# Fp8 rounding in four VectorE operations over a PSUM bank, the clip at the head loads, q/k normalisation on ScalarE, one bank for q/k turns

## The reference

```python
ln_out = ln(layernorm(x)) * ln_w + ln_b
q  = fp8_linear(ln_out, wq)    # 16 heads of 128;  k, v: 8 heads;  qx: 16 heads
kx, vx = split(ctx @ w_kv_x.T) # 8 heads each
q, qx, k, kx = each head normalised over its 128 columns, * weight + bias
core = softmax(q k' / sqrt(128)) v          # 8 groups, 2 query heads per group
xout = softmax(qx kx' / sqrt(128)) vx
catq = fp8(bf16(clip(concat(core, xout) / proj_smooth, -448, 448)))
x = x + catq @ wproj.T * scale
x = x + ffn(layernorm(x))                   # gate/up/down, hidden width 1408
```

## Time and profile before

| | before |
|---|---|
| median of 3 runs | 2063.76 us |
| profiled execution, its own time | 2065.24 us |
| its span | 2063.4 us |
| mean granted TensorE clock | 0.977 |
| PE busy | 1719.0 us (83%) |
| DVE busy | 1648.0 us (80%) |
| ACT busy | 1226.5 us (59%) |
| POOL busy | 1223.0 us (59%) |

### The profile page before, as it was taken

One profiled execution on the slowest core, in us unless ns is written; L12 is line 12 of the kernel. 1 busy time (PEld: TensorE's weight loads), 2 busy tenths in 40 slices (PEclk: granted clock), 3 DMA queues, 4 the chain that ended last, 5 costly groups with the idle time before them and its releaser, 6 DMA issues.

```text
span 2063.4 us, 48409 instructions
## 1 busy us (share of the span) xinstructions
PE 1719.0 (83%) x15776; PEld 1233.5 (60%) x15776; DVE 1648.0 (80%) x3887; ACT 1226.5 (59%) x2158; POOL 1223.0 (59%) x1045
## 2 busy tenths in 40 slices
PE   0016989998998989898889989898999776999998
PEld 0015767776776777676667767776777543444443
DVE  8996999999899989998998999899999732223132
ACT  2244767777666777776677767676788733131211
POOL 3454777777777777777676777776877611120202
PEclk9998999999999999999999999999999888999999
DMA  4100866776777677677867766876788894030200
GB/s 148 40 30 1 139 113 121 150 140 109 124 122 139 116 126 142 118 132 131 139 111 129 141 117 120 136 141 113 124 164 167 189 278 174 6 118 29 93 20 20
DMA packets 639388, 240.92 MB, mean 117 GB/s; under 512 B 612496, under 2 KB 612496, under 8 KB 638608
## 3 DMA queue, kind: packets, MB, share of 16 engines
q1 hardware_dynamic: 639120, 237.62, 57.8%
HBM read 65.57 MB, written 20.97 MB: 42 GB/s over the span
## 4 chain that ended last, share of the span: by engine, by line
DVE 35%; issue 30%; PE 21%; ACT 6%; POOL 3%; SPq 1%; DMA 1%; DVEq 1%; ACTq 0%; POOLq 0%
PE ps_pj L557 8%; DVE local L1050 4%; DVE sq_sum L1121 3%; DVE local L1059 3%; DVE local L1046 3%; DVE local L1178 3%; DVE local L1055 2%; DVE local L1198 2%; POOL local L958 2%; DVE w_raw L1008 2%; DVE local L1140 2%; PE ps_o L626 2%; PE ps_o L628 2%; PE ps_o L627 2%; DVE neg_max L1168 2%
## 5 line engine op out<-in xcount | busy, mean ns | idle before, releaser
L557 PE MATMUL ps_pj<-wide 128*128 (+2 forms) x5544 | 596.5, 256 | 102.6 <-DVE local L1140 82.9
L942 POOL TENSOR_TENSOR local<-local 128x512 bf16<-128x512 f32 x512 | 619.7, 1211 | 78.7 <-ACT local L812 78.3
L557 PEld LDWEIGHTS ps_pj<-wide 128*128 128x128 bf16 x5544 | 466.0, 99 | 250.4 <-DVE local L1140 92.4
L809 ACT ACTIVATE local<-ps_s,neg_max 128x512 f32<-128x512 f32 x512 | 355.1, 693 | 380.8 <-DVE neg_max L1168 378.6
L920 POOL TENSOR_TENSOR head_rstd<-head_var,minus_half 128x3 f32<-128x3 f32 x256 | 247.1, 965 | 339.5 <-DVE head_var L1126 336.8
L626 PE MATMUL ps_o<-v_hi,local 128*128 128x129 bf16 x2048 | 382.9, 224 | 38.4 <-DMA local<-local 25.2
L628 PE MATMUL ps_o<-v_hi,local 128*128 128x129 bf16 x2048 | 382.6, 221 | 0.0
L627 PE MATMUL ps_o<-local 128*128 128x128 bf16 x2048 | 382.2, 220 | 0.0
L1168 DVE TENSOR_REDUCE neg_max<-ps_s 128x1 f32<-128x512 f32 x512 | 344.6, 673 | 44.8 <-PE ps_s L642 42.8
L812 ACT ACTIVATE local<-ps_s,neg_max 128x512 bf16<-128x512 f32 x512 | 352.2, 688 | 15.4 <-DMA local<-local 15.3
L927 POOL TENSOR_TENSOR local<-local 128x512 bf16<-128x512 f32 x192 | 245.9, 1281 | 4.3 <-ACT local L764 4.2
(11 more groups left out here) (99 smaller groups left out, 2866.6 us busy)
## 6 DMA issues: line engine op xcount, KB each, us to landing
w_raw<-w_group SPq DMA_DIRECT2D x32, 512.0 KB, 4.2
quantised_heads<-local SPq DMA_DIRECT2D x32, 512.0 KB, 3.2
wide<-quantised_heads SPq DMA_DIRECT2D x4, 4096.0 KB, 13.8
local<-local SPq DMA_TRANSPOSE x640, 3.3
local<-x SPq DMA_DIRECT2D x4, 1024.0 KB, 5.3
local<-ctx_t SPq DMA_DIRECT2D x4, 1024.0 KB, 5.1
w_raw<-w_proj SPq DMA_DIRECT2D x8, 512.0 KB, 4.1
wide<-w_proj SPq DMA_DIRECT2D x4, 1024.0 KB, 6.2
```

The lines of the kernel that those rows point to most:

```text
L557: last = mm(dst[:, at:at + n], lhs, w_at(par, part, c, cross * 512 + at, n), start=(k == 0), stop=(k == len(terms) - 1))
L809: a(p_exp[:, u % 2], ps_s[u % 2][:], ACT.Exp, bias=neg_max[:, u % 4:u % 4 + 1])
L942: tt_(pp[:, u % PP_BUFS, 1], p_exp[:, u % 2], pp[:, u % PP_BUFS, 0], ALU.subtract)\
```

## The change

- `clip` leaves the slots. The loaded `heads_in` are clipped instead, 128x16384 bf16 in one VectorE operation per batch (`clip_heads`): for batch 0 in slot 65 of the last group, for batches 1 to 3 in the middle of the feed-forward block of the batch before. The output projection waits for `clipped` where it waited for `heads_back`.
- The other four operations: the exponent bits into `mag` (SBUF), max with 2^-6 and min with 256 into the PSUM bank `ps_y` (fp32), and two scalar_tensor_tensor operations that multiply `ps_y` by 24 or -24 and add. Three of them stand at lag 6 and the last at lag 8 (before: 8 and 10); the head's transpose and store are two slots earlier.
- `head_norm` moves from VectorE to ScalarE, as three copies of 128 columns with a per-row scale, behind the exponentials of the odd slot.
- `ps_y` takes the place of the second `ps_qt` bank. Every turn waits for the full copy of the turn before. The bf16 copy stands in the turn's own slot (`QK_LAG` 0), the full copy in the next (`FULL_LAG` 1).
- Weight sums run over six of the eight heads and scaling over seven; the weight steps are one slot later.

```diff
-        ps_qt = [psum(f"ps_qt{i}") for i in range(2)]
+        ps_qt = psum("ps_qt")
+        ps_y = psum("ps_y")
...
-        PV_LAG, Y_LAG, QUANT_LAG, QUANT_END_LAG, HEAD_LAG, STORE_LAG = 5, 6, 8, 10, 11, 13
+        PV_LAG, Y_LAG, HEAD_LAG, STORE_LAG = 5, 6, 9, 11
...
-        QK_LAG, REST_LAG = 1, 3
+        QK_LAG, FULL_LAG, REST_LAG = 0, 1, 3
+        QUANT_LAG, QUANT_END_LAG = 6, 8
...
-        SUMS_LAG, SCALE_LAG, SCALE_PIECES, W_HI_LAG, W_LO_LAG = 2, 4, 2, 8, 10
+        SUMS_LAG, SCALE_LAG, SCALE_PIECES, W_HI_LAG, W_LO_LAG = 3, 5, 2, 9, 11
...
+        CLIP_SLOT = HEADS_SLOT + 6
...
 def turn_qk(q, j, n, tiles):
-                if not isinstance(n, int) or n >= 2:
-                    pe.wait_ge(full_done, n - 1)
+                pe.wait_ge(full_done, n)
...
-                pe.wait_ge(heads_back, 16 * (b + 1))
+                pe.wait_ge(clipped, b + 1)
...
 ScalarE
+            def head_norm(i, t, turns):
+                act.wait_ge(rstd_done, t + 1)
+                if not isinstance(t, int) or t >= TILES:
+                    act.wait_ge(qt_done, turns)
+                for h in range(3):
+                    hs = slice(h * D, (h + 1) * D)
+                    last = a(qn[:, i, hs], tile_bank(i, t)[:, hs], ACT.Copy, scale=head_rstd[:, i % 2, h:h + 1])
+                last.then_inc(qn_done, 1)
...
+            def qk_high(q, j, n):
+                act.wait_ge(qt_done, n + 1)
+                b, cross = quad_place(q)
+                w, bias = qk_columns(q, j)
+                a(qk_hi[:, b, cross, HEAD_OF_TURN[j]], ps_qt[:], ACT.Identity, bias=bias, scale=w)
+
+            def qk_whole(q, j, n):
+                if not isinstance(n, int) or n >= 2:
+                    act.wait_ge(qklo_done, n - 1)
+                w, bias = qk_columns(q, j)
+                a(qk_full[:, (q + j) % 2], ps_qt[:], ACT.Identity, bias=bias, scale=w).then_inc(full_done, 1)
...
 ScalarE, group(), behind the exponentials of the slot
+                    for k in tile_at(slot, QN_LAG, first, last):
+                        head_norm(tile_place(k)[1], GROUP_TILES * g + TILES + k, GROUP_TURNS * g + 3 * (1 + k // TT))
                     for q, j in turn_at(slot, QK_LAG, first, last):
-                        qk_part(q, j, GROUP_TURNS * g + 3 * (2 + q) + j)
+                        qk_high(q, j, GROUP_TURNS * g + 3 * (2 + q) + j)
+                    for q, j in turn_at(slot, FULL_LAG, first, last):
+                        qk_whole(q, j, GROUP_TURNS * g + 3 * (2 + q) + j)
...
 VectorE
+            def clip_heads(b):
+                dve.wait_ge(heads_back, 16 * (b + 1))
+                v.tensor_scalar(heads_in.rearrange("p g h t -> p (g h t)"), heads_in.rearrange("p g h t -> p (g h t)"),
+                                FP8_MAX, -FP8_MAX, ALU.min, ALU.max).then_inc(clipped, 1)
...
                     for H in head_at(slot, QUANT_LAG, first):
-                        binade(B * CH + GROUP_HEADS * g + H, y[:, H % 2], mag)
+                        dve.wait_ge(y_done, SLOTS * g + TT * (H + 1) + UNIT_FREE)
+                        v.tensor_scalar(mag.bitcast(I16), y[:, H % 2].bitcast(I16), EXPONENT, None, ALU.bitwise_and)\
+                            .then_inc(binade_done, 1)
+                        dve.wait_ge(binade_done, GROUP_HEADS * g + H + 1)
+                        v.tensor_scalar(ps_y[:], mag, MIN_BINADE, MAX_BINADE, ALU.max, ALU.min).then_inc(mag_done, 1)
+                        dve.wait_ge(mag_done, GROUP_HEADS * g + H + 1)
+                        v.scalar_tensor_tensor(summed, ps_y[:], KEEP4, y[:, H % 2], ALU.mult, ALU.add).then_inc(total_done, 1)
                     for H in head_at(slot, QUANT_END_LAG, first):
...
+                        v.scalar_tensor_tensor(heads_n[:, H % 2], ps_y[:], -KEEP4, summed, ALU.mult, ALU.add)\
+                            .then_inc(heads_done, 1)
...
 VectorE, hidden()
+                    if m == HC // 2 and clip_next is not None:
+                        clip_heads(clip_next)
```

More of the change, by code:

```diff
@@ L48 @@
 KEEP4 = 24.0
+MAX_BINADE = 256.0
 PP_BUFS = 4
@@ L255, in block_kernel @@
         y_done = sem("y_done")
+        binade_done = sem("binade_done")
+        mag_done = sem("mag_done")
+        total_done = sem("total_done")
+        clipped = sem("clipped")
         heads_done = sem("heads_done")
@@ L750, in v_part, with qk_columns, qk_part @@
                 a(v_hi[:, b % 2, i // TT, i % TT, 0:D], tile_bank(i, t)[:, 3 * D:4 * D], ACT.Copy).then_inc(vhi_done, 1)
-            def qk_part(q, j, n):
+            def head_norm(i, t, turns):
[6 more added lines that the diff above has]
+                last.then_inc(qn_done, 1)
+            def qk_columns(q, j):
+                cross = q % 2
+                if j == 0:
+                    return (c_("kxln_w"), c_("kxln_b")) if cross else (c_("kln_w"), c_("kln_b"))
+                return qscaled[:, 2 * cross:2 * cross + 1], qscaled[:, 2 * cross + 1:2 * cross + 2]
+            def qk_high(q, j, n):
                 act.wait_ge(qt_done, n + 1)
+                b, cross = quad_place(q)
+                w, bias = qk_columns(q, j)
+                a(qk_hi[:, b, cross, HEAD_OF_TURN[j]], ps_qt[:], ACT.Identity, bias=bias, scale=w)
+            def qk_whole(q, j, n):
                 if not isinstance(n, int) or n >= 2:
                     act.wait_ge(qklo_done, n - 1)
[L757 to L764, removed]
+                w, bias = qk_columns(q, j)
+                a(qk_full[:, (q + j) % 2], ps_qt[:], ACT.Identity, bias=bias, scale=w).then_inc(full_done, 1)
+            def qk_part(q, j, n):
+                qk_high(q, j, n)
+                qk_whole(q, j, n)
             scale_chunk(B - 1, 0)
@@ L779, in _ @@
                     v_part(0, i, i)
+                    head_norm(i - 1, i - 1, 0)
                 if i == START_TURN:
@@ L782, in _ @@
                         qk_part(-2, j, j)
+            head_norm(TILES - 1, TILES - 1, 0)
             for j in range(3):
@@ L996, in weight_sums @@
                 dve.wait_ge(w_loaded, 16 * (count + FREE))
[L997 removed]
+                v.tensor_reduce(w_sum[:].rearrange("p (s k) -> p s k", s=2)[:, :, 0:3],
+                                raw(c).rearrange("p (s k d) -> p s k d", s=2, k=4)[:, :, 0:3], AX_X, ALU.add).then_inc(w_step, 1)
                 dve.wait_ge(w_step, 2 * count - 1)
@@ L1005, in weight_scale @@
                 n = 8 // SCALE_PIECES
-                for k in range(n * piece, n * (piece + 1)):
+                for k in range(n * piece, min(n * (piece + 1), 7)):
                     head = raw(c)[:, k * D:(k + 1) * D]
@@ L1133, in v_rest @@
                                 v_hi[:, b % 2, i // TT, i % TT, 0:D], ALU.subtract).then_inc(vlo_done, 1)
[L1135 to L1143, removed]
             quantise_chunk(B - 1, 0, True)
@@ L1169, in group @@
                             .then_inc(max_done, 1)
-                    for H in head_at(slot, QUANT_LAG, first):
-                        clip(B * CH + GROUP_HEADS * g + H, y[:, H % 2])
                     for u in unit_at(slot, Y_LAG, first):
@@ L1189, in group @@
                         head_variance(tile_place(k)[1], GROUP_TILES * g + TILES + k)
[L1190 to L1198, removed]
                     for piece in range(SCALE_PIECES):
@@ L1208, in group @@
                         v.reciprocal(rows, rows).then_inc(smooth_ready, 1)
+                    if last and slot == CLIP_SLOT:
+                        clip_heads(0)
             group(0, True, False)
@@ L1241, in output, with hidden @@
                     v.tensor_tensor(y_out[:, tt % 2], scaled[:, tt % 2], x1_at(b, tt), ALU.add).then_inc(out_ready, 1)
-            def hidden(b):
+            def hidden(b, clip_next):
                 for tt in range(TT):
@@ L1255, in hidden @@
                                            ALU.mult, ALU.mult).then_inc(hid_done, 1)
+                    if m == HC // 2 and clip_next is not None:
+                        clip_heads(clip_next)
             residual(0, [*EARLY_BANKS, ps_s[EARLY_TILES % 2]])
-            hidden(0)
-            with dve.Fori(1, B) as b:
+            hidden(0, 1)
+            with dve.Fori(1, B - 1) as b:
                 residual(b, ps_s * 2)
                 output(b - 1)
-                hidden(b)
+                hidden(b, b + 1)
+            residual(B - 1, ps_s * 2)
+            output(B - 2)
+            hidden(B - 1, None)
             output(B - 1)
```

16 lines of the change are left out of this document (8 added, 8 removed).

## The result

The changed kernel took 2230.83 us (median, 2227.8 to 2237.54), the kernel before 2065.02 us beside it: a ratio of 1.08, 95% interval 1.0763 to 1.0838. The direction was forecast, the size was not: 2160 us was forecast with a range to 2220, and +166 us was measured against +96.

A forecast was written before the change was run, and what follows sets the result against it. VectorE was taken to bound the kernel before, and a serial chain through ScalarE the changed one. Main stage +86, start +5, first clip +4 and other clips +1 gave +96 us, so 2160 us, range 2085 to 2220.

The forecast's parts named there:

- VectorE's relief: Main stage: moving head_norm and cheaper rounding cut VectorE's work from 176 to about 144 us per group.
- The chain: Serial waits from scores through ScalarE's exponentials and copies to scores two slots on: 189.2 us per group.
- what comes on top of the chain: Main-stage extras per group: 3.4 us on VectorE plus 4.5 us, making a group 197.1 us.
- late work on VectorE: VectorE late for a maximum: 2.4 us at the slot-31 reciprocal plus 1 us for weight pieces, per group.
- the rest: Return of the loop to its first slot and late transposes: 4.5 us per group (0 to 6).
- Weight pieces that meet a rounding add 1 us: VectorE in the main stage: weight steps meeting rounding operations make it late, 1 us more per group.
- the reciprocal: Slot 31 on VectorE: about 7.6 us of work against a 5.2 us pair, so 2.4 us late per group.
- The share of the stage: Seven and a half groups feel the +11.5 us per group, the first and last only partly: +86 us.
- Start and end: Outside the loop: start +5 us from serialised turns and head_norm on ScalarE, first clip +4, other clips +1.
- Clip: Clip of 16384 loaded columns on VectorE: 6.4 us each; batch 0 costs +4 us, the other three +1 in all.
- VectorE's relief decides: Rival: ScalarE's part released a slot early, TensorE bounds the stage; -117 us, 1947 us, pair under 5.7 us; chance 0.14.
- Extras vanish: Rival: the loop binds but its extras hide in slack and waits; group 189 to 191 us, 2101 us; chance 0.19.

The follow-up runs named there:

- the first two experiments: Changed kernel with the full q/k copy moved ahead of ScalarE's exponentials: 2167.09 us; with the three normalising copies moved ahead as well: 2053.80 us.
- the third: Kernel before with only the normalisation moved to ScalarE behind the exponentials, two turn banks and five rounding operations kept: 2146.14 us, ratio 1.0377.
- the last but one experiment: Changed kernel with full and normalising copies ahead of the exponentials, weight steps at their earlier lags, reciprocal in four pieces: 1999.60 us, ratio 0.967.
- the kernel without the collisions: Changed kernel with the weight steps at their lags of before and the reciprocal in four pieces: 2162.48 us.

## Why the prediction was right in direction and wrong in size

- *VectorE's relief.* Forecast from 176 to 144 us of busy time per group; measured 77% of 205.9 = 159. The work itself was forecast well: the summed durations of its instructions fell by 29.5 us per group (208.8 to 179.3), where 32 was forecast. The rounding came out at 2.70 us per head (2.96 taken), and the weight scales rose from 340 to 540 ns each. The busy time fell less because neighbours overlap only 21.5 us per group now, against 33.2 before. As a sum this load bound nothing; where its pieces stand did cost, as the next points say.
- *The chain.* Right for the changed kernel, to 1 us in 190, and shown twice by taking links out (the first two experiments) and once by putting one link into the kernel before (the third). What the chain becomes without the full copy I had wrong: 5.79 us for the later turns, 5.23 measured.
- *The failed step: what comes on top of the chain.* I took 3.4 us for late work on VectorE and 4.5 for the rest; 15.7 were measured. The term "Weight pieces that meet a rounding add 1 us" had no rows behind it and was mis-sized most: 5.8. Of these, 4.9 us lie in the pairs that shrink when the weight steps go back (12, 18, 24, 28, 44); 0.9 (8, 48, 56) stay and were not explained. For the reciprocal the working set VectorE's load in a slot against the length of its pair (2.4, measured 4.0). It left out what stands ahead of the maximum at the moment when the scores end: the weight sums stand at the head of their slot, the low part of the weights behind a rounding block, and the delay that they leave goes onto the chain. It also left the prices of the weight steps as they were, while the new places put them beside GpSimd's subtractions. Putting the weight steps back alone took 7.5 us per group.
- *A price with no term at all.* TensorE idle ahead of the half clock, and then TensorE's part of the chain at half clock. Where the pairs 28 and 44 had such a stretch of 3.4 us they were 1.4 to 1.65 us longer than without. In all it cost 3.4 us per group. It goes away with the collisions (10.2 us of half clock to 1.7, all of it at the start of the group), so it is a consequence of them; that the idle time itself brings it down was not tested by itself.
- *The share of the stage.* I let the first group count three quarters. It lost 22.2 us (175.8 to 198.0), more than the mean of the loop: 13 us of the miss. The six looped groups make 53 of it.
- *Start and end.* Start +5.8 (forecast 5). From the first score of the last group to the end +17.2 (13.6 forecast with three quarters of a group). Clip: 4.42 us measured, 6.4 taken, and no cost seen.
- *The rivals.* "VectorE's relief decides" did not happen in the change; in another order of ScalarE's list (the last but one experiment) a gain appears, 69 us where this rival had 117, with a pair at 174.9 / 32 = 5.47 us, under the 5.7 from which it was to decide. "Extras vanish" was the wrong way round.

## What to carry to other kernels

When work moves off the busiest engine, look at what stands ahead of it in the new engine's list, and who waits for it: write the chain from one product to the same product two slots on, with every link, before any sum of loads. A chain that binds has no slack: of an item that stands ahead of one of its links, what is left to do when the link could start goes onto the time, and an engine's summed load says nothing of it. An item that is moved by one slot can also get another price from what runs beside it. Put what others wait for, and whose inputs are early, ahead of what waits for a fresh result.

## What the runs showed of the hardware

A scalar_tensor_tensor of 128x512 with one input in PSUM took 0.69 us and with both in SBUF 1.17 and 1.00 us on the mean, beside a busy GpSimd. A bf16 max/min of 128x512 in SBUF took 0.29 us, or 1.12 to 1.14 us beside a GpSimd subtraction; written to PSUM it took 0.70 us either way. The weight scale of 128x128 (L1043) took 0.33 us at best and up to 1.19 us beside a GpSimd subtraction, and never more than 0.37 us beside GpSimd's reciprocal root, with the weight steps at their lags of before. ScalarE's 128-column copy from PSUM with a pointer scale started its successor 0.25 us later and lasted 0.38 us. TensorE's granted clock stayed at 2.4 GHz for all but 1.7 us per group in the kernel without the collisions, where gaps over 2 us stood only where one group meets the next, and was at 1.2 GHz for 19.9 us per group in the kernel with the binades in SBUF, with gaps of up to 3.39 us.
